# A convolution kernel on one core: the VectorE order of tile 3 interleaved in smaller pieces, and a split matmul taken out of all tiles but one

## The chip, the core and the metric

The kernel runs on one core of a Trainium2 chip. The metric is the device time of one execution in microseconds (us). The engines are TensorE (PE, with its weight loads shown apart as PEld), VectorE (DVE), ScalarE (ACT), GpSimd (POOL) and the DMA queues (SP's and POOL's among them).

## What is computed

The input `x` has 16 images of 256 channels and 56x56 pixels, in fp32.

```
v   = group_norm(x, 32 groups)                   # 8 channels to a group, mean and variance of each
h   = gelu(depthwise_conv3x3(v, dw_weight))      # 9 taps, zero padding
maps = pw_weight @ h + pw_bias                   # 256 -> 8 x 256 channels, for each pixel
out = x + sum_i maps[i] * (roll(v, offset_i) - v)   # 8 directions
```

## The kernel before

An image is worked in 7 tiles of 8 rows (448 pixels), for both halves of the channels (2 x 128). A body covers two images (14 tiles, `nl` from 0 to 13, `t = nl % 7`), and the bodies run one after the other. All engines run the same tiles by hand-written orders, held together by semaphores.

TensorE (`make_maps`) makes the eight direction maps of a tile in 8 units `u`. A unit is two maps ("sides") of 128x448 in two PSUM banks; each map takes six matmuls, since weights and activations are split in a high and a low part (hi x hi, hi x lo, lo x hi, for two halves of the input channels). That is 12 matmuls for a unit, 96 for a tile, 672 for an image. Three units fit in PSUM (MAP_GROUPS = 3), so unit q waits until VectorE has consumed unit q-3: the first wait of `make_maps`, on `prod_s`. The weight load of a matmul is issued ahead of it, so this wait shows at the weight load.

ScalarE (`add_bias`, line 587) scales each map and adds its bias. Between units it also computes gelu for a later tile (line 569), the centre tap that starts a later tile's convolution (`start_conv`, lines 555 and 559), and the cast to the high part (line 574).

VectorE consumes the units: units 0 and 1 by `first_product` (line 702), unit 2 by `second_product` (line 702, in place in PSUM) and `second_add` (line 724, it waits for the product), units 3 to 7 by `kept_product` (line 702, into `products`), which GpSimd adds to the sums (line 363). Between the products VectorE puts in the other eight taps of the convolution of the tile three steps ahead (`tap`, line 784). The seventh tile of an image (SINGLE) holds 8 rows of both channel halves where the others pair two tiles of one half, so its eight taps are sixteen half taps (line 775), two for each call of `tap`. Its taps fall into tile t = 3. Into the same tile (STATS_TILE = 3) fall eleven small operations in nine steps, `group_stats` (lines 656 to 682), which turn the next image's moments into group statistics: each step waits for the one before on VectorE itself. In the last image there is no next image, and tile 3 has no statistics.

VectorE's order in a tile, by `stats_next` (next step of the statistics, nothing where there is none) and `tap_next`, is before: both first products, stats, stats, tap, stats, second product, second add, stats, tap, stats, product 3, stats, tap, stats, product 4, stats, tap, stats, product 5, tap, product 6, tap, tap, product 7, tap. The fourth stats step has two subtractions with the same inputs and different outputs (lines 665 and 666), because the fifth multiplies them with each other (line 669).

TensorE's matmuls are whole (448 columns), but for two places: one matmul of unit 2 in the very first tile (HALVED_FIRST), and one of unit 3 in tile 4 of every image (HALVED) are issued as two matmuls of 224 columns that do the same work.

Of the kernel before, what the change touches and what calls it, by code (L numbers as in the profile page):

```python
# [5 lines left out]
def preact_directional_conv(nc, x, pw_t, pw_b, dw, out):  # L6

    F32, F32R = mybir.dt.float32, mybir.dt.float32r
    ALU, ACT, AX = mybir.AluOpType, mybir.ActivationFunctionType, mybir.AxisListType

    P = 128
    B, C, H, W = x.shape
# [56 lines left out]
    with ctx:  # L69
# [154 lines left out]
        TPAIRS = TILES // 2  # L224
        HALF_STEPS = 2 * SLICES + 2
        MEASURES = HALVES * HALF_STEPS
        STAT = 11
        SCALES = 3
        CONSTS = 5
        PB_SUMS = 5  # L230
# [7 lines left out]
        def upto(table, b0, c):  # L238


            return b0 * sum(table) + ((c // CSTEPS) * sum(table) + sum(table[:c % CSTEPS]))
# [396 lines left out]
        def _(dve):  # L638
            def group_stats(b):


                done = [0]

                def then(ins):
                    ins.then_inc(stat, 1)
                    done[0] += 1

                def wait():

                    dve.wait_ge(stat, b * STAT + done[0])  # L650

                by8 = lambda v: v.rearrange("p (a e) -> p a e", e=GROUP)
                wide = lambda v: window(v, [[1, 32 // GROUP], [0, GROUP]])

                dve.wait_ge(measure, b * MEASURES + MEASURES)
                then(nc.vector.transpose(mom_t[:], moments[:]))
                yield
                wait()
                then(nc.vector.reduce_sum(sums[:], by8(mom_t[:]), axis=AX.X))
                yield  # L660
                wait()
                then(nc.vector.tensor_scalar(by8(mean_t), wide(sums[:]), 1.0 / GROUP, None, ALU.mult))
                yield
                wait()
                then(nc.vector.tensor_tensor(dev_t, mom_t[:], mean_t, ALU.subtract))
                then(nc.vector.tensor_tensor(dev_s[:], mom_t[:], mean_t, ALU.subtract))
                yield
                wait()
                then(nc.vector.tensor_tensor(dev_t, dev_t, dev_s[:], ALU.mult))
                yield  # L670
                wait()
                then(nc.vector.reduce_sum(sums[:], by8(dev_t), axis=AX.X))
                yield
                wait()
                then(nc.vector.tensor_scalar(by8(devs_t), wide(sums[:]), 1.0 / GROUP, None, ALU.mult))
                yield
                wait()
                then(nc.vector.transpose(mean_b[:], mean_t))  # L678
                then(nc.vector.transpose(devs_b, devs_t))  # L679
                yield  # L680
                wait()
                then(nc.vector.scalar_tensor_tensor(var_eps[:], mean_b[:, 1:4:2], EPS, devs_b[:, 0:3:2],
                                                    ALU.add, ALU.add))
                yield
# [49 lines left out]
            def last_tile(n0, nl):  # L734
# [8 lines left out]
                for u in range(HALVES, UNITS):  # L743
# [13 lines left out]
                    if u >= UNITS - HALVES:  # L757
                        dve.wait_ge(prod_s, n * UNITS + u + 1 + PROD0)
                        nc.vector.tensor_tensor(products[:, g, 0, :], a[:, g, 0], a[:, g, 1],
                                                ALU.add).then_inc(final_s, 1)  # L760

            def tap(n0, b0, c, j):


                ip, s, g, t = step_of(c)
                conv = conv_of(n0, c)
                ky, kx = divmod(TAPS_DVE[j], 3)
                if s == SINGLE:
                    for g in range(HALVES):
                        if j == 0:  # L770
                            dve.wait_ge(start_s, upto(START_OF, b0, c) + (g + 1))
                        else:
                            dve.wait_ge(tap_s, upto(TAPS_OF, b0, c) + (2 * (j - 1) + g + 1))
                        d = conv[:, g, :].rearrange("p (r c) -> p r c", c=W)
                        nc.vector.scalar_tensor_tensor(  # L775
                            d, xn[c % 2][:, g * TR + ky:g * TR + ky + ROWS, kx:kx + W],
                            dw_f[:, g, TAPS_DVE[j]:TAPS_DVE[j] + 1], d, ALU.mult, ALU.add).then_inc(tap_s, 1)
                    return
                if j == 0:
                    dve.wait_ge(start_s, upto(START_OF, b0, c + 1))  # L780
                else:
                    dve.wait_ge(tap_s, upto(TAPS_OF, b0, c) + j)
                d = conv.rearrange("p a (r c) -> p a r c", c=W)
                nc.vector.scalar_tensor_tensor(  # L784
                    d, xn[c % 2][:, ky:ky + 2 * ROWS, kx:kx + W].rearrange("p (a r) c -> p a r c", a=2),
                    dw_f[:, g, TAPS_DVE[j]:TAPS_DVE[j] + 1], d, ALU.mult, ALU.add).then_inc(tap_s, 1)
# [56 lines left out]
            def stats_next():  # L843
                for _step in itertools.islice(stats, 1):
                    pass

            def body(n0, b0, last):
                nonlocal stats
                for nl in range(STEPS):
                    t, par = nl % TILES, nl // TILES  # L850
                    taps = iter(range(NT) if not (last and nl + 3 >= STEPS) else ())

                    def tap_next():
                        for j in itertools.islice(taps, 1):
                            tap(n0, b0, nl + 3, j)

                    if last and nl == STEPS - 1:
                        last_tile(n0, nl)
                        return


                    first_product(n0, nl, 0)
                    first_product(n0, nl, 1)
                    if t == STATS_TILE and not (last and par):
                        stats = iter(group_stats(b0 + par + 1))
                    stats_next()
                    stats_next()
                    tap_next()
                    stats_next()
                    second_product(n0, nl)  # L870
                    second_add(n0, nl)
                    stats_next()
                    tap_next()
                    stats_next()
                    kept_product(n0, nl, 3)
                    stats_next()
                    tap_next()
                    stats_next()
                    kept_product(n0, nl, 4)
                    stats_next()  # L880
                    tap_next()
                    stats_next()
                    kept_product(n0, nl, 5)
                    tap_next()
                    kept_product(n0, nl, 6)
                    tap_next()
                    tap_next()
                    kept_product(n0, nl, 7)
                    tap_next()
# [3 lines left out]
        @block.tensor  # L893
        def _(pe):

            HALVED_FIRST = (0, 2, 0, 2)
            HALVED = (4, 3, 0, 2)

            def make_maps(n0, nl, u):

                t, q = nl % TILES, nl * UNITS + u

                need = nl + (1 if t == TILES - 1 else 2)
                wanted = t % 2 == 0


                pe.wait_ge(prod_s, n0 * UNITS + (q - MAP_GROUPS + 1 + PROD0))
                if u == 0 and wanted:
                    pe.wait_ge(hhi_s, n0 + need)
                for side in range(2):  # L910
                    d, g = unit_map(u, side)
                    col = d * C + g * P
                    steps = [(w, hhi, kk) for kk in range(HALVES) for w in (w_hi, w_lo)]
                    steps += [(w_hi, hlo, kk) for kk in range(HALVES)]
                    for s, (w, h, kk) in enumerate(steps):
                        if u == 0 and side == 0 and s == 2 * HALVES and wanted:
                            pe.wait_ge(hlo_s, n0 + need)
                        cuts = (0, PX)
                        if (t, u, side, s) == HALVED or (n0 + nl, u, side, s) == HALVED_FIRST:
                            cuts = (0, PX // 2, PX)  # L920
                        for x0, x1 in itertools.pairwise(cuts):
                            last = nc.tensor.matmul(maps(n0 * UNITS + q)[:, side, x0:x1], w[:, kk, col:col + P],  # L922
                                                    h_part(h, t, nl, kk)[:, x0:x1],
                                                    start=s == 0, stop=s == len(steps) - 1)
                    last.then_inc(maps_s, 1)

            pe.wait_ge(w_lo_s, 1)

            def body(n0, b0, last):
                for nl in range(STEPS):  # L930
                    for u in range(UNITS):
                        make_maps(n0, nl, u)

            run(body)
# [26 lines left out]
```

## Time and profile before

| | us |
|---|---|
| median of 3 runs | 2215.76 |
| lowest, highest | 2214.11, 2215.88 |
| the profiled execution, device time | 2214.68 |
| its span, first to last instruction | 2212.9 |
| busy TensorE, VectorE, GpSimd, ScalarE | 2158.2, 2067.0, 1978.2, 1839.9 |
| mean granted TensorE clock | 0.999 |

The span is 1.8 us shorter than the device time of the same execution. Busy times are sums of instruction durations; a busy TensorE is not TensorE at its peak, and matmuls overlap in the pipeline, so their distance from start to start is what counts, not the duration. All times in the rows count from the span's start.

### The profile page before, as it was taken

To read this page: it belongs to the slowest core of one execution; us is meant where nothing else is said; L and a number is where in the kernel's file an instruction comes from. 1 tells how busy PE (TensorE), PEld (TensorE's weight loads), DVE (VectorE), ACT (ScalarE), POOL (GpSimd) and SP (SyncE) were. 2 spreads that over 40 slices of the span, in tenths; PEclk is the share of its full clock that TensorE was granted. 3 is DMA by queue.
4 is the path that set the end of the run, shared out by engine and by line. 5 is a ranking of instruction groups with operands and counts; after the bars stand their busy time and mean duration, and the time that the engine had idled before them with its cause. 6 is when DMAs were issued, how large, how long until landed. Compare 5 with 4: busy or idle time off the path is not lost.

```text
span 2212.9 us, 28734 instructions
## 1 busy us (share of the span) xinstructions
PE 2158.2 (98%) x10769; PEld 2019.3 (91%) x10769; DVE 2067.0 (93%) x2234; ACT 1839.9 (83%) x2762; POOL 1978.2 (89%) x857
## 2 busy tenths in 40 slices
PE   1999999999999999999999999999999999999998
PEld 1999999999999999999999999999999999999998
DVE  7999999999999999999999999999999999999996
ACT  5979889798887988889788897988879888797775
POOL 5799899899989999899898998999989998999985
PEclk9999999999999999999999999999999999999999
DMA  6245264443725437254462644536354372543424
GB/s 183 48 79 129 48 113 99 89 103 51 157 52 107 92 60 159 34 109 100 70 139 35 124 98 81 114 50 131 79 94 98 60 164 35 108 101 51 100 34 75
DMA packets 47083, 202.13 MB, mean 91 GB/s; under 512 B 3040, under 2 KB 7136, under 8 KB 45664
## 3 DMA queue, kind: packets, MB, share of 16 engines
q0 software_dynamic: 30192, 94.97, 26.3%
q1 hardware_dynamic: 16752, 105.34, 18.6%
q8 instruction: 84, 1.38, 0.3%
q14 instruction: 55, 0.45, 0.1%
HBM read 104.88 MB, written 146.80 MB: 114 GB/s over the span
## 4 chain that ended last, share of the span: by engine, by line
PE 84%; DVE 11%; ACT 2%; issue 2%; DMA 0%; POOL 0%; SPq 0%; DVEq 0%; ACTq 0%
PE psum L922 84%; DVE psum L775 4%; DVE products L702 3%; DVE psum L702 1%; ACT psum L587 1%; DVE psum L784 1%; ACT psum L555 1%; DVE acc L724 1%; ACT hid L569 1%; DMA acc<-x 0%; DVE acc L756 0%; POOL hlo L332 0%; DVE mean_b L678 0%; DVE psum L679 0%; DVE fields L807 0%
## 5 line engine op out<-in xcount | busy, mean ns | idle before, releaser
L587 ACT ACTIVATE psum<-psum,bias,rstd 128x448 f32<-128x448 f32 x1792 | 1200.1, 694 | 323.7 <-PE psum L922 320.5
L922 PE MATMUL psum<-hhi,w_hi 128*128 128x448 f32 x3601 | 1301.9, 362 | 47.0 <-ACT hhi L574 45.3
L363 POOL TENSOR_TENSOR acc<-acc,products 128x896 f32<-128x896 f32 x333 | 1165.8, 3501 | 162.1 <-DVE products L702 150.0
L922 PE MATMUL psum<-hhi,w_lo 128*128 128x448 f32 x3584 | 1300.2, 363 | 0.0
L922 PE MATMUL psum<-hlo,w_hi 128*128 128x448 f32 x3584 | 1009.0, 363 | 0.3 <-POOL hlo L332 0.3
L784 DVE SCALAR_TENSOR_TENSOR psum<-xn,dw_f,psum 128x896 f32<-128x896 f32 x768 | 881.3, 1148 | 72.3 <-ACT psum L559 66.7
L922 PEld LDWEIGHTS psum<-hhi,w_hi 128*128 128x128 f32 x3601 | 676.7, 188 | 97.0 <-issue 45.3
L922 PEld LDWEIGHTS psum<-hlo,w_hi 128*128 128x128 f32 x3584 | 673.2, 188 | 44.9 <-POOL hlo L332 0.9
L922 PEld LDWEIGHTS psum<-hhi,w_lo 128*128 128x128 f32 x3584 | 673.4, 188 | 43.9
L702 DVE TENSOR_TENSOR products<-psum,fields 128x896 f32<-128x896 f32 x555 | 600.6, 1082 | 14.7 <-ACT psum L587 11.1
L332 POOL TENSOR_TENSOR hlo<-hid,hhi 128x896 fp32r<-128x896 f32 x112 | 264.5, 2362 | 12.8 <-ACT hhi L574 12.8
L702 DVE TENSOR_TENSOR acc<-psum,fields 128x896 f32<-128x896 f32 x224 | 241.4, 1085 | 13.8 <-ACT psum L587 12.2
L348 POOL TENSOR_TENSOR fields<-xpad 128x896 f32<-128x896 f32 (+1 forms) x112 | 239.8, 2141 | 0.0
L344 POOL TENSOR_TENSOR fields<-xpad 128x912 f32<-128x912 f32 (+1 forms) x112 | 210.0, 1875 | 0.0
L775 DVE SCALAR_TENSOR_TENSOR psum<-xn,dw_f,psum 128x448 f32<-128x448 f32 x256 | 160.6, 676 | 2.5 <-ACT psum L555 0.5
L702 DVE TENSOR_TENSOR psum<-psum,fields 128x896 f32<-128x896 f32 x117 | 128.6, 1099 | 17.4 <-ACT psum L587 10.1
L370 POOL DMA_DIRECT2D out<-acc x111 | 132.5, 1193 | 7.5 <-DMA out<-acc 6.9
L724 DVE TENSOR_TENSOR acc<-psum,acc 128x896 f32<-128x896 f32 x111 | 121.2, 1092 | 11.9 <-DVE psum L702 0.5
L569 ACT ACTIVATE hid<-psum 128x896 f32<-128x896 f32 x112 | 102.3, 913 | 20.8 <-DVE psum L784 12.6
L540 ACT ACTIVATE xn<-xpad,shift,rstd 128x1008 f32<-128x1008 f32 (+1 forms) x96 | 116.7, 1215 | 0.0
L574 ACT CAST hhi<-hid 128x896 fp32r<-128x896 f32 x112 | 104.8, 935 | 0.0
L559 ACT ACTIVATE psum<-xn,dw_f 128x896 f32<-128x896 f32 x96 | 97.6, 1016 | 8.7
(67 smaller groups left out, 448.2 us busy)
## 6 DMA issues: line engine op xcount, KB each, us to landing
out<-acc POOLq DMA_DIRECT2D x96, 896.0 KB, 7.7
out<-x SPq DMA_DIRECT2D x16, 3136.0 KB, 12.9
xpad<-x SPq DMA_DIRECT2D x30, 1568.0 KB, 14.8
out<-acc POOLq DMA_DIRECT2D x15, 448.0 KB, 5.6
acc<-x SPq DMA_DIRECT2D x4, 784.0 KB, 6.7
xpad<-pw_t SPq DMA_DIRECT2D x1, 2048.0 KB, 12.1
out<-products SPq DMA_DIRECT2D x2, 224.0 KB, 1.9
dw_f<-dw SPq DMA_DIRECT2D x1, 9.0 KB, 8.1
```

Of the source, the lines that this page charges most:

```text
L332: nc.gpsimd.tensor_tensor(hlo[:, slot], hid[:], hhi[:, slot].bitcast(F32), ALU.subtract).then_inc(hlo_s, 1)
L344: nc.gpsimd.tensor_tensor(gx[:, :, f + 2 * lo:f + TR, :], v[:, :, r + 2 * lo:r + TR, 1:WP], v[:, :, r + 2 * lo:r + TR, 0:WP - 1], ALU.subt ...
L348: nc.gpsimd.tensor_tensor(gy[:, :, f + lo:f + ROWS + 1, :], v[:, :, r + lo + 1:r + TR, 1:W + 1], v[:, :, r + lo:r + ROWS + 1, 1:W + 1], AL ...
L363: nc.gpsimd.tensor_tensor(a, a, p, ALU.add).then_inc(added_s, 1)
L370: pool.dma_start(out_dst[b, :, :, t * PX:(t + width) * PX], acc[buf][:, :, sign].rearrange("p g t x -> p g (t x)"), accum_op=ALU.add).then ...
L569: nc.scalar.activation(hid[:], conv_of(n0, c), ACT.Gelu).then_inc(gelu_s, 1)
L587: nc.scalar.activation(m, m, ACT.Identity, bias=bias[ip][:, g, d:d + 1], scale=rstd[ip][:, g:g + 1]).then_inc(biased_s, 1)
L702: return nc.vector.tensor_tensor(to.rearrange("p s (r c) -> p s r c", c=W), maps(n0 * UNITS + q).rearrange("p s (r c) -> p s r c", c=W), f ...
L724: nc.vector.tensor_tensor(a, maps((n0 + nl) * UNITS + u), a, ALU.add).then_inc(prod_s, 1)
L775: nc.vector.scalar_tensor_tensor(d, xn[c % 2][:, g * TR + ky:g * TR + ky + ROWS, kx:kx + W], dw_f[:, g, TAPS_DVE[j]:TAPS_DVE[j] + 1], d, A ...
L784: nc.vector.scalar_tensor_tensor(d, xn[c % 2][:, ky:ky + 2 * ROWS, kx:kx + W].rearrange("p (a r) c -> p a r c", a=2), dw_f[:, g, TAPS_DVE[ ...
L922: last = nc.tensor.matmul(maps(n0 * UNITS + q)[:, side, x0:x1], w[:, kk, col:col + P], h_part(h, t, nl, kk)[:, x0:x1], start=s == 0, stop= ...
```

## The change

Three things are changed. In the single tile (t = 3) the half taps come one at a time: the order up to the second add is now stats, half tap, stats, half tap, stats, half tap, second product, stats, second add, half tap; from there on it is as before, with two half taps for each tap. In the statistics the subtraction is done once, into `dev_s`, and the multiplication squares it: ten operations where there were eleven. The matmul of unit 3 in tile 4 is whole again; the split one in the first tile stays. In other tiles the calls of `stats_next` up to the second add are gone, where they issued nothing.

```diff
-        STAT = 11
+        STAT = 10
...
-                then(nc.vector.tensor_tensor(dev_t, mom_t[:], mean_t, ALU.subtract))
                 then(nc.vector.tensor_tensor(dev_s[:], mom_t[:], mean_t, ALU.subtract))
                 yield
                 wait()
-                then(nc.vector.tensor_tensor(dev_t, dev_t, dev_s[:], ALU.mult))
+                then(nc.vector.tensor_tensor(dev_t, dev_s[:], dev_s[:], ALU.mult))
...
+            def half_tap(n0, b0, c, j, g):
+
+                conv, ky, kx = conv_of(n0, c), *divmod(TAPS_DVE[j], 3)
+                if j == 0:
+                    dve.wait_ge(start_s, upto(START_OF, b0, c) + (g + 1))
+                else:
+                    dve.wait_ge(tap_s, upto(TAPS_OF, b0, c) + (2 * (j - 1) + g + 1))
+                d = conv[:, g, :].rearrange("p (r c) -> p r c", c=W)
+                nc.vector.scalar_tensor_tensor(
+                    d, xn[c % 2][:, g * TR + ky:g * TR + ky + ROWS, kx:kx + W],
+                    dw_f[:, g, TAPS_DVE[j]:TAPS_DVE[j] + 1], d, ALU.mult, ALU.add).then_inc(tap_s, 1)
...
                     def tap_next():
                         for j in itertools.islice(taps, 1):
                             tap(n0, b0, nl + 3, j)
+                        half_tap_next()
+                        half_tap_next()
...
-                    stats_next()
-                    stats_next()
-                    tap_next()
-                    stats_next()
-                    second_product(n0, nl)
-                    second_add(n0, nl)
-                    stats_next()
-                    tap_next()
+                    if single:
+                        stats_next()
+                        half_tap_next()
+                        stats_next()
+                        half_tap_next()
+                        stats_next()
+                        half_tap_next()
+                        second_product(n0, nl)
+                        stats_next()
+                        second_add(n0, nl)
+                        half_tap_next()
+                    else:
+                        tap_next()
+                        second_product(n0, nl)
+                        second_add(n0, nl)
+                        tap_next()
                     stats_next()
                     kept_product(n0, nl, 3)
...
-            HALVED = (4, 3, 0, 2)
...
-                        if (t, u, side, s) == HALVED or (n0 + nl, u, side, s) == HALVED_FIRST:
+                        if (n0 + nl, u, side, s) == HALVED_FIRST:
                             cuts = (0, PX // 2, PX)
```

## Rows read from the trace of the kernel before

**Rows 1.** The page, busy time of each engine over the whole span
```profile
PE 2158.2 (98%) x10769; PEld 2019.3 (91%) x10769; DVE 2067.0 (93%) x2234; ACT 1839.9 (83%) x2762; POOL 1978.2 (89%) x857
```

**Rows 2.** The waits of the whole span: who waited for whom, total, times, longest
```profile
PEld psum L922 <- DVE products L702: 7.2, 15, 0.5
```

**Rows 3.** The chain of waits: start us, us, what (pieces in order of time)
```profile
399.71 115.52 PE psum L922 x577
...
804.18 115.59 PE psum L922 x577
```

**Rows 4.** TensorE timeline, third image: start us, us, form, count, idle before
```profile
399.03 0.56 PE L922 MATMUL psum<-hlo,w_hi 128*128 128x448 f32 x2
399.71 0.47 PE L922 MATMUL psum<-hhi,w_hi 128*128 128x448 f32 x1
400.01 0.36 PE L922 MATMUL psum<-hhi,w_lo 128*128 128x448 f32 x1
...
402.21 0.36 PE L922 MATMUL psum<-hhi,w_hi 128*128 128x448 f32 x1
...
402.61 0.38 PE L922 MATMUL psum<-hhi,w_hi 128*128 128x224 f32 x2
...
403.85 0.36 PE L922 MATMUL psum<-hhi,w_hi 128*128 128x448 f32 x1
```

**Rows 5.** Timeline of the weight loads at the same place
```profile
399.70 0.19 PEld L922 LDWEIGHTS psum<-hhi,w_hi 128*128 128x128 f32 x1 [0.48 <-DVE products L702]
```

**Rows 6.** TensorE timeline, sixth delay: twelve matmuls apart
```profile
804.69 0.37 PE L922 MATMUL psum<-hhi,w_hi 128*128 128x448 f32 x1
...
807.17 0.38 PE L922 MATMUL psum<-hhi,w_hi 128*128 128x224 f32 x2
```

**Rows 7.** TensorE by kind in the window 270 to 390 us
```profile
L922 PE MATMUL psum<-hhi,w_lo 128*128 128x448 f32 x200 | 72.5, 363 | 0.0
```

**Rows 8.** VectorE timeline in tile 3 of the third image
```profile
382.74 1.28 DVE L775 SCALAR_TENSOR_TENSOR psum<-xn,dw_f,psum 128x448 f32<-128x448 f32 x2
383.93 0.18 DVE L662 TENSOR_SCALAR psum<-sums 128x32 f32<-128x32 f32 x1
384.53 1.10 DVE L702 TENSOR_TENSOR psum<-psum,fields 128x896 f32<-128x896 f32 x1 [0.42 <-ACT psum L587]
385.73 1.09 DVE L724 TENSOR_TENSOR acc<-psum,acc 128x896 f32<-128x896 f32 x1
386.74 0.18 DVE L665 TENSOR_TENSOR psum<-mom_t,psum 128x32 f32<-128x32 f32 x1
...
386.93 1.27 DVE L775 SCALAR_TENSOR_TENSOR psum<-xn,dw_f,psum 128x448 f32<-128x448 f32 x2
...
388.22 1.07 DVE L702 TENSOR_TENSOR products<-psum,fields 128x896 f32<-128x896 f32 x1
...
398.58 1.07 DVE L702 TENSOR_TENSOR products<-psum,fields 128x896 f32<-128x896 f32 x1
...
400.76 1.07 DVE L702 TENSOR_TENSOR acc<-psum,fields 128x896 f32<-128x896 f32 x1
```

**Rows 9.** ScalarE timeline in the same tile
```profile
380.43 0.70 ACT L587 ACTIVATE psum<-psum,bias,rstd 128x448 f32<-128x448 f32 x1 [0.50 <-PE psum L922]
...
382.06 1.20 ACT L555 ACTIVATE psum<-xn,dw_f 128x448 f32<-128x448 f32 x2
383.20 1.29 ACT L587 ACTIVATE psum<-psum,bias,rstd 128x448 f32<-128x448 f32 x2
```

**Rows 10.** TensorE timeline: unit 5 of tile 3 starts
```profile
387.43 0.36 PE L922 MATMUL psum<-hhi,w_hi 128*128 128x448 f32 x1
```

**Rows 11.** TensorE timeline at the start of the kernel
```profile
49.80 0.92 PE L922 MATMUL psum<-hlo,w_hi 128*128 128x448 f32 x2
50.54 0.38 PE L922 MATMUL psum<-hhi,w_hi 128*128 128x448 f32 x1
...
53.36 0.38 PE L922 MATMUL psum<-hhi,w_hi 128*128 128x224 f32 x2
```

More of the change, by code:

```diff
@@ L767, in tap @@
                 ky, kx = divmod(TAPS_DVE[j], 3)
[L768 to L778, printed above, removed]
                 if j == 0:
@@ L850, in body, with half_tap_next @@
                     t, par = nl % TILES, nl // TILES
-                    taps = iter(range(NT) if not (last and nl + 3 >= STEPS) else ())
+                    single = (nl + 3) % CSTEPS == SINGLE
+                    taps = iter(range(NT) if not single and not (last and nl + 3 >= STEPS) else ())
+                    half_taps = iter(itertools.product(range(NT), range(HALVES)) if single else ())
+                    def half_tap_next():
+                        for j, g in itertools.islice(half_taps, 1):
+                            half_tap(n0, b0, nl + 3, j, g)
                     def tap_next():
@@ L863, in body @@
                     first_product(n0, nl, 1)
+                    assert single == (t == STATS_TILE)
                     if t == STATS_TILE and not (last and par):
                         stats = iter(group_stats(b0 + par + 1))
-                    stats_next()
-                    stats_next()
-                    tap_next()
-                    stats_next()
-                    second_product(n0, nl)
-                    second_add(n0, nl)
-                    stats_next()
-                    tap_next()
+                    if single:
[14 more added lines that the diff above has]
+                        tap_next()
                     stats_next()
```

## The prediction

> **What bounds the kernel now.** I read the busy times first: TensorE is busy for 98% of the span [rows 1], so nothing that another engine saves counts unless it moves TensorE's stream. So the next view is the waits, and there TensorE's own line. After it has started it waits for VectorE 15 times, 7.2 us in total and never over 0.5 us [rows 2]: once for each image that has statistics to make. The chain of waits says the same: TensorE carries it in pieces of 577 matmuls, one for each image, that begin right behind such a wait [rows 3].
>
> The timeline of the third image shows the place. Matmuls start 0.20 us apart; 601 start between 270 and 390 us, so the pace is 0.2000 us (the row has one of the three kinds, 200 of them, the others have 201 and 200) [rows 7]. The two matmuls from 399.03 on should be followed by one at 399.43, and it starts at 399.71; the next comes 0.30 us behind it instead of 0.20 [rows 4]. The loss is 0.27 + 0.11 = 0.38 us. It is unit 2 of tile 4, whose weight load waited 0.48 us [rows 5] for the product of unit 7 of tile 3, which ends at 398.58 + 1.07 = 399.65 [rows 8]. So VectorE's chain through tile 3, the one tile with sixteen half taps and the statistics, is what is late. From the end of the product to the weight load it is 0.05 us, and in the steady stream the load starts 0.20 us ahead of its matmul, so a product must end about 0.25 us ahead of its matmul to cost nothing. The very next unit shows that 0.38 us is enough: the product it waits for ends at 400.76 + 1.07 = 401.83 [rows 8], and its first matmul starts at 402.21, eleven matmuls and 2.20 us behind 400.01, exactly on pace [rows 4].
>
> A second thing is to be seen in TensorE's stream: it has two paces. After the delay at 804.18 us the matmuls start 2.48 us / 12 = 0.2067 us apart, until the split matmul at 807.17 [rows 6]; from there on it is 0.2000 again. The stretches of the chain with the slow pace in them last 115.59 instead of 115.52 us [rows 3], 4 of the 15; after the other eleven delays the fast pace is back within a few matmuls. So a delay may leave the stream 6.67 ns slow for each matmul, and the split matmul, whatever its reason, stands where the slow pace ends.
>
> **The change, part by part.** All times are those of the third image.
>
> The start of the chain doesn't move. The bias of unit 1 waits for TensorE (0.50 us idle before 380.43), gelu and the two centre taps follow; the two centre taps take 1.20 us from 382.06, so the first ends near 382.7 [rows 9]. The first half tap starts at 382.74 [rows 8]: it waits for that centre tap, and the small steps ahead of it lie in this wait. TensorE sets this time, so everything below can be counted against TensorE's pace.
>
> From there to product 3 it takes 388.22 - 382.74 = 5.48 us now. New: a half tap occupies VectorE for 0.59 us (two in 383.93 - 382.74 = 1.19), a small operation for 0.10 (two from 386.74 to 386.93) [rows 8]. Half tap 382.74, stats 383.34, half tap 383.43 (its centre tap is done at 383.26), stats 384.02, half tap 384.12, second product 384.71. The bias of unit 2 is done at 383.20 + 1.29 = 384.49 [rows 9], so it is no longer waited for; now the product waits for it until 384.53 [rows 8]. The second product gets 0.18 later. The add waits for it: start to start 385.73 - 384.53 = 1.20, against 386.74 - 385.73 = 1.01 behind an operation that nothing waits for [rows 8]. So the fourth small step, put between, fits into that 0.19 and costs nothing; if its cover were gone it would cost 0.10. Add at 385.92, half tap 386.93, stats 387.52, product 3 at 387.62. The gain is 388.22 - 387.62 = 0.60 us: 0.41 of idle time filled by the third half tap, 0.10 hidden behind the second product, 0.10 of the operation removed. The biases of units 3 to 7 leave room: the three that start after the cast end well before, and later ones are paced by TensorE.
>
> From product 3 on the order is the same, so product 7 ends at 399.65 - 0.60 = 399.05. Its matmul is due at 399.43: 0.38 ahead, and 0.25 is needed. The delay of 0.38 us goes, in all 15 images, and unit 3's product is then also earlier against its matmul (0.60 gained, 0.38 given back by the stream). What is next in line: unit 5 of tile 3, which waits for the second add. The add ends at 385.73 + 1.09 = 386.82 now and 387.01 then, its matmul is due at 387.43 [rows 10]: 0.42 ahead. Tile 4's gelu waits for the last half tap, now 0.60 earlier.
>
> The trace has a wait of VectorE for its own last result as 0.19 us of extra distance. The Trainium skill, "VectorE: DVE Perf Modes", section "The DRAIN you can't avoid", says that a semaphore between chained operations costs nothing extra. By that rule the hidden step would gain nothing: product 7 would end 0.28 us ahead of its matmul, and a delay of some images would be as likely as not. The rows speak against it here.
>
> The split matmul: 402.61 to 403.85 holds six matmuls' work and takes 1.24 us [rows 4], so it costs 0.04 us, 16 times. Taking it out also takes out what ends the slow pace. Where no delay comes, no slow pace starts: from the split matmul of the first tile at 53.36 us on [rows 11] this trace keeps 0.2000 to the first delay.
>
> The prologue makes the first statistics on the path to the first matmul: one of two subtractions goes, at the 0.10 us that it takes up in tile 3 [rows 8], once, with nothing beside it. No DMA and no step on SP's or GpSimd's queue moves. GpSimd's power step and its adds get their inputs 0.6 us earlier, and they are not on the chain.
>
> Sum: 15 x 0.38 = 5.7; four slow stretches x 0.07 = 0.3; 16 x 0.04 = 0.6; prologue 0.1; together 6.7 us. On the profiled execution's own 2214.68 that is 2208.0. The median of the runs is 1.1 above that execution and the lowest 0.6 below; since the profiled one lies between them I put the new median at **2208.6**. The unknown part is small: with no gain in the prologue and 0.37 for a delay it is 6.4, with 0.40 it is 7.0, and the runs spread by 1.8.
>
> **The rivals.**
>
> First: the delay stays, smaller, and the slow pace has nothing to end it (slower). It decides at VectorE gaining under 0.47 us in tile 3 where I have 0.60, for instance if half taps beside small steps take longer than in pairs. Then a slow pace lasts from one delay to the next: 656 more matmuls x 6.67 ns = 4.4 us. At the share seen (4 of 15) that is 17.5 us against 0.7 saved: 2214.7 - 0.7 + 17.5 = 2231.5; if every delay fell badly, 2214.7 - 0.7 + 66 = 2280. For it: the reserve is only 0.13 us, and unit 5 of tile 3 has but 0.17. Against it: the 15 delays are alike, and 0.38 cost nothing at unit 3.
>
> Second: the slow pace comes with the clock's rise, not with a delay (slower). Up to 50.54 us matmuls of 448 columns lie 0.37 us apart (two in 50.54 - 49.80), which fits the clock's lower level of 1.2 GHz (448 columns / 1.2 GHz = 0.373) though no row shows a granted clock below full there; from then on they are 0.20 apart, at the upper level of 2.4 GHz, and the split matmul of the first tile stands at 53.36 [rows 11]. If in a run the clock rose behind it, the pace could stay slow: before, the next split matmul at tile 4 ended that (about 400 x 6.67 ns = 2.6 us); now nothing does, and 10,700 x 6.67 ns = 71 us makes 2279. Against it: the split lies 2.8 us behind the rise, and the runs before spread by less than 2.6.
>
> Third: the delays stay in part or whole and the pace stays fast (about the same). With all of them it is 2214.7 - 0.7 - 0.3 = 2213.7, with half 2210.9. The Trainium skill, "TensorE: Matmul & The Clock Gate", section "Wait — 56ns, not 53.3ns?", has one warm distance, columns / 2.4 GHz + 2.5 ns, an estimated 189 ns here. By that rule a delay leaves no trace and a split matmul serves nothing, and this case takes the whole place of the first rival. The rows have 200 and 207 ns, two paces.
>
> **How the numbers follow.** The forecast gets 0.80, the first rival 0.08, the second 0.04, the third 0.08. The forecast's own range is 2207 to 2210; the range reaches to half of the third case, 2206.5 to 2212. A measurement of this kernel can tell about 0.2%, or 4.4 us, from no change: faster means under 2211.3. Faster: 0.80 + half of the third, 0.84; same 0.04; slower 0.12.
>
> **What would show it.** In the profile after: no row of weight loads waiting for VectorE; the chain of waits as one TensorE piece of over 10,000 matmuls; product 7 of tile 3 ending 0.3 to 0.4 us before the matmul of unit 2 of tile 4; second product about 0.2 us later against TensorE and product 3 0.6 earlier; matmuls 0.2000 us apart throughout. The prediction is wrong if a delay of any size is left, above all with 0.2067 us behind it.

## The result: slower, 2234.1 us, and the profile after

The changed kernel takes 2234.09 us (median of 5 runs, 2226.54 to 2240.50) against 2215.54 before (2214.11 to 2215.88). The ratio is 1.0085, with a 95% interval of 1.0072 to 1.0098. The forecast was 2208.6 us, and the delays of TensorE that were to go are twice as many. The profiled execution took 2235.41 us. The mean granted clock was 0.999 in all five runs.

The waits of the whole span of the changed kernel, the lines that answer [rows 2]: who waited for whom, total, times, longest.

```profile
PEld psum L938 <- DVE products L701: 19.2, 30, 0.9
...
DVE psum L769 <- ACT psum L555: 5.6, 15, 0.5
...
PE psum L938 <- DVE products L701: 8.9, 22, 0.5
```

TensorE now waits for VectorE twice in each of 15 images: at unit 6 of tile 3 (for product 3) and at unit 2 of tile 4 (for product 7), where before there was one wait of 0.5 us at most. In the third image, the weight loads show it (start us, us, engine, what; in brackets the wait):

```profile
394.58 0.19 PEld L938 LDWEIGHTS psum<-hhi,w_hi 128*128 128x128 f32 x1 [0.30 <-DVE products L701]
...
404.94 0.19 PEld L938 LDWEIGHTS psum<-hhi,w_hi 128*128 128x128 f32 x1 [0.82 <-DVE products L701]
```

The timeline of VectorE in tile 3 of the third image, which answers [rows 8], shows which step is late; behind it stands GpSimd's timeline at the same place. Columns: start us, us, engine, line, operation, output and inputs.

```profile
387.39 0.69 DVE L769 SCALAR_TENSOR_TENSOR psum<-xn,dw_f,psum 128x448 f32<-128x448 f32 x1 [0.36 <-ACT psum L555]
...
389.36 1.09 DVE L701 TENSOR_TENSOR psum<-psum,fields 128x896 f32<-128x896 f32 x1
390.36 0.18 DVE L665 TENSOR_TENSOR dev_s<-mom_t,psum 128x32 f32<-128x32 f32 x1
390.56 1.09 DVE L723 TENSOR_TENSOR acc<-psum,acc 128x896 f32<-128x896 f32 x1
391.56 0.68 DVE L769 SCALAR_TENSOR_TENSOR psum<-xn,dw_f,psum 128x448 f32<-128x448 f32 x1
392.15 1.38 DVE L668 TENSOR_TENSOR psum<-dev_s 128x32 f32<-128x32 f32 x1
393.45 1.08 DVE L701 TENSOR_TENSOR products<-psum,fields 128x896 f32<-128x896 f32 x1
```

```profile
389.58 1.80 POOL L348 TENSOR_TENSOR fields<-xpad 128x896 f32<-128x896 f32 x1
391.35 2.12 POOL L332 TENSOR_TENSOR hlo<-hid,hhi 128x896 fp32r<-128x896 f32 x1
```

Everything up to the square is as forecast: from the first half tap to the square it is 392.15 - 387.39 = 4.76 us, and the prediction had 387.52 - 382.74 = 4.78. Then the square of 32 numbers (line 668), which the prediction booked at 0.10 us, lasts 1.38 us. It ends at 393.53; GpSimd's subtraction ends at 391.35 + 2.12 = 393.47. In the group view all sixteen squares together take 24.2 us:

```profile
L668 DVE TENSOR_TENSOR psum<-dev_s 128x32 f32<-128x32 f32 x16 | 24.2, 1513 | 0.0
```

The one in the prologue lasts 0.20 us (no GpSimd operation runs there). The other fifteen last 1.0 to 1.9 us, and all fifteen end about 0.06 us behind the end of the GpSimd operation that was running (line 332). The line before, which multiplied a PSUM tensor with an SBUF tensor at the same place, took 0.19 us beside the same GpSimd operation. The half tap at 391.56 reads `xn` and its weights `dw_f` from SBUF, with a PSUM tensor as third input, and takes its usual 0.68 us while the same GpSimd operation runs; `dw_f` gives it one number for each partition and not a second tensor.

The chain of waits, answering [rows 3], shows what the delays do to TensorE's pace (start us, us, matmuls):

```profile
130.16 132.96 PE psum L938 x642
...
812.12 128.92 PE psum L938 x642
...
2032.58 188.76 PE psum L938 x912
```

Pieces of 642 matmuls take 128.92 or 132.96 us, that is 0.2008 or 0.2071 each. The distances of matmul starts over the whole trace say how much each part costs: all distances of the slow pace in stretches (1732 of them, in two long ones of 622 and 934 and some short) cost 1732 x 6.67 ns = 11.6 us, and the 30 delays with the longer distance behind each cost 16.2 us. Together this is 27.8 us.

### The profile page after: what moved, and what is told of

The parts are those of the page before. It is cut to its first block, busy times and chain, and to the rows that moved or that the text cites. A ratio compares the mean times of both kernels' runs of the same rounds, so it can differ in the third digit from the quotient of the medians.

```text
span 2233.6 us, 28686 instructions
## 1 busy us (share of the span) xinstructions
PE 2172.1 (97%) x10753; PEld 2014.1 (90%) x10753; DVE 2083.6 (93%) x2218; ACT 1840.6 (82%) x2762; POOL 1978.2 (89%) x857
## 3 DMA queue, kind: packets, MB, share of 16 engines
q8 instruction: 84, 1.38, 0.3%
## 4 chain that ended last, share of the span: by engine, by line
PE 88%; DVE 9%; ACT 1%; issue 1%; DMA 0%; POOL 0%; SPq 0%; ACTq 0%; DVEq 0%
PE psum L938 88%; DVE psum L769 4%; DVE products L701 2%; DVE psum L784 1%; DVE psum L668 1%; DVE psum L701 0%; DMA acc<-x 0%; ACT hid L569 0%; ACT psum L587 0%; DVE acc L723 0%; ACT psum L555 0%; DVE acc L755 0%; POOL hlo L332 0%; DVE fields L807 0%; DVE part_sums L794 0%
## 5 line engine op out<-in xcount | busy, mean ns | idle before, releaser
L701 DVE TENSOR_TENSOR products<-psum,fields 128x896 f32<-128x896 f32 x555 | 601.3, 1083 | 16.2 <-ACT psum L587 13.1
```

The lines of the kernel that those rows point to most:

```text
L701: return nc.vector.tensor_tensor(to.rearrange("p s (r c) -> p s r c", c=W), maps(n0 * UNITS + q).rearrange("p s (r c) -> p s r c", c=W), f ...
```

## The experiments

The theory from this profile: the square reads two inputs from SBUF and is held until the running GpSimd operation ends; this makes the delays longer; and without the split matmul each delay may leave the slow pace for long. The rivals: the new order or the close spacing of small steps makes VectorE late; the square is slow for another reason; the slow pace costs nothing that a split matmul mends.

**Two subtractions again, new order and whole matmul kept.**

```diff
-        STAT = 10
+        STAT = 11
...
+                then(nc.vector.tensor_tensor(dev_t, mom_t[:], mean_t, ALU.subtract))
                 then(nc.vector.tensor_tensor(dev_s[:], mom_t[:], mean_t, ALU.subtract))
...
-                then(nc.vector.tensor_tensor(dev_t, dev_s[:], dev_s[:], ALU.mult))
+                then(nc.vector.tensor_tensor(dev_t, dev_t, dev_s[:], ALU.mult))
```

> The changed kernel with the old statistics: two subtractions again, and the product of the PSUM copy with the SBUF copy. The order in half taps and the whole matmul stay. Theory (the square of an SBUF tensor with itself takes two SBUF inputs and waits for the GpSimd instruction that runs, 1.0 to 1.9 us in the trace after): the multiplication lasts 0.19 us again, product 3 comes 0.6 us earlier than before, all 15 delays go, time 2207.5 to 2210. Rival (the new order itself, or waits between close small steps, makes VectorE late): the delays stay as in the changed kernel, 2226 to 2240.

Measured: 2207.79 us (7 runs, 2207.04 to 2208.76) beside 2214.33 before, ratio 0.9971 (0.9960 to 0.9982). The profiled execution took 2207.58. The one operand makes the difference between 2234 and 2208. Its chain of waits is one piece of TensorE, and its VectorE timeline in the third image has the multiplication at its old length beside the same GpSimd operation:

```profile
47.17 2146.35 PE psum L939 x10725
```

```profile
383.41 1.09 DVE L702 TENSOR_TENSOR psum<-psum,fields 128x896 f32<-128x896 f32 x1
384.41 0.18 DVE L665 TENSOR_TENSOR psum<-mom_t,psum 128x32 f32<-128x32 f32 x1
384.50 0.18 DVE L666 TENSOR_TENSOR dev_s<-mom_t,psum 128x32 f32<-128x32 f32 x1
384.61 1.09 DVE L724 TENSOR_TENSOR acc<-psum,acc 128x896 f32<-128x896 f32 x1
385.62 0.68 DVE L770 SCALAR_TENSOR_TENSOR psum<-xn,dw_f,psum 128x448 f32<-128x448 f32 x1
386.20 0.19 DVE L669 TENSOR_TENSOR psum<-psum,dev_s 128x32 f32<-128x32 f32 x1
386.30 1.08 DVE L702 TENSOR_TENSOR products<-psum,fields 128x896 f32<-128x896 f32 x1
```

```profile
385.38 2.13 POOL L332 TENSOR_TENSOR hlo<-hid,hhi 128x896 fp32r<-128x896 f32 x1
```

Both subtractions fit between the second product and the add: add 1.20 us behind the product, as with no step between [rows 8]. The changed kernel's profiled execution is 2235.4 - 2207.6 = 27.8 us longer than this one, which is what the delays and the slow pace add up to above.

**The square alone, in the kernel before.** The edit is the statistics part of the change by itself: STAT 10, the first subtraction gone, `dev_s` multiplied with itself.

> The kernel before with the one-subtraction statistics alone; old order, the split matmul in every image kept. Theory: the square starts 0.68 to 1.25 us ahead of the end of GpSimd's split of h and lasts that long plus 0.06, so VectorE is 0.5 to 1.0 us later in tile 3 and each of 15 delays grows from 0.38 by that; with the split matmul there the slow pace stays under 50 matmuls an image. 2215.5 + 15 x 0.75 = 2227, range 2222 to 2232. Rival (the square costs nothing by itself): 2215.

Measured: 2227.16 us (4 runs, 2226.26 to 2227.69), ratio 1.0057 (1.0044 to 1.0070). In the third image the square lasts 0.83 us, until 0.06 behind GpSimd's end at 388.84 + 2.12 = 390.96. It lasts 0.83 us in seven images, 1.40 in seven and 1.13 in one. TensorE waits at weight loads 30 times, 19.5 us.

```profile
390.19 0.83 DVE L668 TENSOR_TENSOR psum<-dev_s 128x32 f32<-128x32 f32 x1
```

```profile
388.84 2.12 POOL L332 TENSOR_TENSOR hlo<-hid,hhi 128x896 fp32r<-128x896 f32 x1
```

**The changed kernel with the split matmul back.**

```diff
+            HALVED = (4, 3, 0, 2)
...
-                        if (n0 + nl, u, side, s) == HALVED_FIRST:
+                        if (t, u, side, s) == HALVED or (n0 + nl, u, side, s) == HALVED_FIRST:
```

> The changed kernel with the split matmul of unit 3 in tile 4 of every image back. Theory (two paces): the profiled execution of the changed kernel had 1732 matmuls at 0.2067 us, 11.6 us of its time, in two long stretches of 622 and 934; with the split matmul no stretch is longer than about 60 matmuls, so about 11 us less and 0.6 more for the split: 2222 to 2226, and the runs spread by less than 3 us instead of 14. Rival (the split matmul does nothing but cost 0.04 us): 2234, with the same spread.

Measured: 2227.26 us (5 runs, 2226.50 to 2227.76), ratio 1.0057 (1.0045 to 1.0069). The spread fell from 14 us to 1.3, as expected of the two paces. The median was expected at 2222 to 2226 and lies above: in the profiled execution the slow stretches still cost 1.7 us, where 0.04 x 16 = 0.6 for the splits was all that I had added. It equals the experiment before it, which differs in the order alone, and the two traces show why: the new order brings VectorE to the square earlier, but the square ends with the same GpSimd operation, and all that follows counts from there. In the third image the square ends at 390.19 + 0.83 = 391.02 with the old order and the delayed matmul of tile 4 starts at 402.43; with the new order it ends at 388.62 + 1.36 = 389.98 and the matmul starts at 401.40, 11.41 and 11.42 us behind.

```profile
388.62 1.36 DVE L668 TENSOR_TENSOR psum<-dev_s 128x32 f32<-128x32 f32 x1
```

```profile
401.40 0.47 PE L939 MATMUL psum<-hhi,w_hi 128*128 128x448 f32 x1 [0.33 <-DVE products L701]
```

**The kernel before without the split matmul.** The reverse of that edit, on the kernel before.

> The kernel before without the split matmul of unit 3 in tile 4; all else as before. Theory: 15 delays of 0.38 us stay, and each leaves the slow pace for 656 more matmuls, 4.4 us, with a chance of about 4 in 15: 2215.5 - 0.6 + 17.5 = 2232, range 2219 to 2250, with runs some us apart. Rival (one pace): 2214.9, runs within 2 us.

Measured: 2260.20 us median of 7 runs from 2223.92 to 2277.02. (The ratio of 1.013 that comes with it, 1.0085 to 1.0175, leaves out the four longest of them, so the runs themselves are what to read.) The slow pace is there, and worse than expected. The chain of waits of its profiled execution (2260.2 us):

```profile
533.78 115.51 PE psum L921 x576
668.60 1577.55 PE psum L921 x7632
```

After the fifth delay the slow pace came and stayed for the rest, 7652 distances, 51 us. There is no sixth delay: all waits of weight loads for VectorE are five, 2.4 us. At 0.2067 us a tile takes 96 x 6.67 ns = 0.64 us longer, more than the 0.48 that TensorE waited [rows 5], so VectorE is not late again, and no delay comes that could give the fast pace another chance. The trace bears this out: in the ten later images with statistics product 7 ends 0.42 us ahead of its matmul, where the prediction needs 0.25. The rows are those of the eleventh image (1500.46 + 1.09 = 1501.55, matmul at 1501.97). The granted clock from 700 to 2200 us is 1.00, as in the same stretch of the kernel before, so the slow pace is not a lower clock. That the runs differ by when the stream falls into the slow pace fits this, but only one of them has a trace.

```profile
1500.46 1.09 DVE L702 TENSOR_TENSOR products<-psum,fields 128x896 f32<-128x896 f32 x1
```

```profile
1501.97 0.37 PE L921 MATMUL psum<-hhi,w_hi 128*128 128x448 f32 x1
```

**Two SBUF copies against one SBUF and one PSUM copy.** Both kernels have the new order, two subtractions and the split matmul in every image. They differ in where the first subtraction writes. The reference:

> The new order with two subtractions as in the first experiment, and the split matmul in every image too. With no delay there is no slow pace for the split to end, so all it does is cost 0.04 us 16 times: 2207.8 + 0.6 = 2208.4, within 2207.5 to 2209.5. It is also the reference for the next one, which differs in one operand. Rival (the split matmul saves something even without a delay): under 2207.

Measured: 2208.51 us (7 runs, 2208.22 to 2209.81) beside 2215.20 before, ratio 0.9971 (0.9960 to 0.9981); no wait of TensorE for VectorE. Its median is 0.7 us above that of the first experiment, but the two ran on different occasions, and each is about as far below its own before (6.7 and 6.5 us). The traces tell what 16 splits cost: from the split in the first tile to the start of the last matmul it is 2198.85 - 53.19 = 2145.66 us here and 2197.94 - 52.91 = 2145.03 in the first experiment, 0.63 more, and 16 x 0.04 is 0.64.

The other kernel differs from it so:

```diff
+        dev_u = sb("dev_u", [P, 32])
...
-                then(nc.vector.tensor_tensor(dev_t, mom_t[:], mean_t, ALU.subtract))
+                then(nc.vector.tensor_tensor(dev_u[:], mom_t[:], mean_t, ALU.subtract))
...
-                then(nc.vector.tensor_tensor(dev_t, dev_t, dev_s[:], ALU.mult))
+                then(nc.vector.tensor_tensor(dev_t, dev_u[:], dev_s[:], ALU.mult))
```

> The same, but both subtractions write SBUF tensors, and two different SBUF tensors are multiplied. Theory (a VectorE operation with two SBUF inputs waits for the running GpSimd operation, whatever they are): the multiplication lasts 1.0 to 1.9 us, ending about 0.06 us behind GpSimd's split of h, 30 waits of TensorE, 2226 to 2228 as the changed kernel with the split back. Rival (it is reading one tensor through both inputs that is slow, or reading what was just written): 2208.4.

Measured: 2227.77 us (4 runs, 2227.38 to 2228.00), ratio 1.0056 (1.0041 to 1.0072). Two different tensors, and the same wait, to the same end. So it is not the squaring of one tensor:

```profile
390.16 1.35 DVE L670 TENSOR_TENSOR psum<-dev_u,dev_s 128x32 f32<-128x32 f32 x1
```

```profile
389.33 2.12 POOL L333 TENSOR_TENSOR hlo<-hid,hhi 128x896 fp32r<-128x896 f32 x1
```

**One subtraction, without a second SBUF input.**

```diff
-                then(nc.vector.tensor_tensor(dev_s[:], mom_t[:], mean_t, ALU.subtract))
+                then(nc.vector.tensor_tensor(dev_t, mom_t[:], mean_t, ALU.subtract))
...
-                then(nc.vector.tensor_tensor(dev_t, dev_s[:], dev_s[:], ALU.mult))
+                then(nc.vector.tensor_tensor(dev_t, dev_t, mom_t[:], ALU.mult))
```

> The changed kernel with one subtraction, into PSUM, multiplied with the SBUF moments instead of with itself: since deviations of a group sum to zero, the sum of deviation times value is the sum of squared deviations. Ten operations, and one SBUF input beside a PSUM one. Theory: this is what the prediction described, 2207.5 to 2208 (0.1 us of the prologue less than with two subtractions); the multiplication lasts 0.19 us and no wait of TensorE for VectorE is left. Rival (something in the count of operations or their spacing matters): over 2212.

Measured: 2207.73 us (5 runs, 2207.52 to 2207.97), ratio 0.9967 (0.9954 to 0.9979). The multiplication lasts 0.19 us:

```profile
386.47 0.19 DVE L668 TENSOR_TENSOR psum<-psum,mom_t 128x32 f32<-128x32 f32 x1
```

That no wait is left holds but for one: in the eleventh image the second add starts 0.36 us late, for no reason that the profile shows, and the weight load of unit 5 of tile 3, which the prediction had named as next in line, waits 0.17 us for it:

```profile
1461.57 0.19 PEld L938 LDWEIGHTS psum<-hhi,w_hi 128*128 128x128 f32 x1 [0.17 <-DVE acc L723]
```

This kernel has all that the change set out to do, and it and the first experiment beat both kernels. Between these two no difference can be told.

**No split matmul anywhere, no delay.** The first experiment, with the split of the first tile taken out as well.

> The first experiment (two subtractions, no delay left) without the split matmul of the first tile. Theory (the clock's rise leaves either pace, and without a split or a delay it stays to the end): profiles so far show the slow pace between the clock's rise and the first split in 3 of 6 executions. So about half the runs near 2207.5 and about half near 2207.8 + 10,740 x 6.67 ns = 2279, nothing between. Rival (only delays bring the slow pace, or it ends by itself): all runs within 2 us of 2207.8.

Measured: six runs: 2207.60, 2207.88, 2208.00, 2208.39, 2208.42 and 2279.06 us. The sixth value is within 0.4 us of the forecast for a whole kernel at the slow pace, and there is nothing between. The share was one in six instead of half; six runs don't fix it. The profiled execution was one of the quick ones, so no trace shows the long one: that it is the slow pace rests on its length and on the traces above. Its mean granted clock was 1.000, so a lower clock did not make it long. In the nine profiled executions that have the split of the first tile, the pace between what the prediction calls the clock's rise (where the distances go from 0.37 to 0.20 us) and that split was slow in four.

## Why the prediction was wrong

**What bounds the kernel** was read rightly: a delay of 0.38 us at one place, for product 7 of tile 3, and two paces. The first experiment removed the delays and landed at 2207.8 where the forecast was 2208.6; it is 6.5 us less than its own before, where the sum had 6.7.

**The step that failed** is "stats 387.52, product 3 at 387.62": I priced the new multiplication at the 0.10 us of every small operation, by rows of operations that had at most one SBUF input. The change removed "0.10 of the operation removed" and, with it, the PSUM copy that was the second operand. The runs showed 1.0 to 1.9 us instead, the rest of a GpSimd operation of 2.1 us. From the first half tap to product 3 the third image now takes 393.45 - 387.39 = 6.06 us, where it took 5.48 before and 4.88 was forecast. So VectorE was 0.6 us later where it was to be 0.6 earlier. This put a new delay at unit 6 of tile 3, and longer ones at tile 4: 16.2 us in place of 5.7.

The Trainium skill states this, and I did not weigh it: "SBUF — State Buffer", section "Who interferes with whom", has a VectorE instruction with two SBUF inputs contend with a GpSimd instruction that reads SBUF, since the second input comes through an interface that both share, and the later one waits for the other to finish. The traces agree: in the changed kernel all fifteen ends lie about 0.06 us behind GpSimd's, and so do the fifteen in each of the other three traces with two SBUF inputs. In all of them the GpSimd operation is the same one, the subtraction that makes `hlo`; no run tries another.

The trace of the kernel before has what fits it, from the other side, in rows that the prediction did not use. In the prologue VectorE joins the weights, SBUF with SBUF, and GpSimd's small operations beside it are long:

```profile
18.96 1.03 POOL L320 TENSOR_TENSOR rstd<-var_eps,neg_half 128x2 f32<-128x2 f32 x1 [6.28 <-DVE var_eps L682]
20.07 0.60 POOL L323 TENSOR_TENSOR shift<-mean_b,rstd 128x2 f32<-128x2 f32 x1
20.64 0.66 POOL L324 TENSOR_TENSOR bias<-pb_f,rstd 128x16 f32<-128x16 f32 x1
```

The same three take 0.71, 0.19 and 0.21 us in tile 3:

```profile
123.55 0.71 POOL L320 TENSOR_TENSOR rstd<-var_eps,neg_half 128x2 f32<-128x2 f32 x1 [1.70 <-DVE var_eps L682]
124.34 0.19 POOL L323 TENSOR_TENSOR shift<-mean_b,rstd 128x2 f32<-128x2 f32 x1
124.50 0.21 POOL L324 TENSOR_TENSOR bias<-pb_f,rstd 128x16 f32<-128x16 f32 x1
```

**The order** was right term by term. The second product comes 0.2 later, steps between it and the add are free, and the chain from the first half tap to the step after is 4.76 us against 4.78. With the old operands, product 7 ends 0.39 us ahead of its matmul (396.67 + 1.08 = 397.75, matmul at 398.14 in the third image) where 0.38 was forecast:

```profile
396.67 1.08 DVE L702 TENSOR_TENSOR products<-psum,fields 128x896 f32<-128x896 f32 x1
```

```profile
398.14 0.36 PE L939 MATMUL psum<-hhi,w_hi 128*128 128x448 f32 x1
```

So the hidden small step is hidden, as the rows had said. The Trainium skill's rule that a semaphore between chained operations costs nothing extra ("VectorE: DVE Perf Modes", section "The DRAIN you can't avoid"), which the prediction cites, does not hold at this place: 1.20 us from start to start with the wait, 1.01 without it [rows 8].

**The first rival** came true in its second half, a slow pace that nothing ends. Its first half had a smaller delay left, from half taps beside small steps; the delays grew instead, and by the square. Its price was mis-sized too. I let the slow pace last from one delay to the next, 4.4 us; with delays of 0.38 us it ends the delays too and stays, 51 us in the trace of the kernel before without its split. With the longer delays of the changed kernel VectorE is late even for the slow stream, so each delay decides the pace anew, and the slow one costs 11.6 us. Forecast for this case: 2231.5; measured: 2234.1. That the two are near is luck: the rival had 17.5 us of slow pace with no new delays, the profiled execution has 11.6 of it and 10.5 more of delays (16.2 - 5.7).

**The second rival**, a slow pace from the clock's rise on, has its start shown by the four traces above. That the clock is what rises there is inferred from the distances: the granted clock of the kernel before is 1.00 on both sides (45 to 49 and 51 to 60 us). That it can last to the end rests on the length of one run of six, 2279.06 against the 2279 worked out, and it showed only once the first tile's split was gone too. The changed kernel keeps that split, and in its profiled execution the split did end a slow pace, at 52.60 us.

**The third rival**, delays without a lasting slow pace, is ruled out by the same runs: taking out one split matmul for each image moved the kernel before by 46 us (2260.20 - 2214.33). The Trainium skill's rule of one warm distance ("TensorE: Matmul & The Clock Gate", section "Wait — 56ns, not 53.3ns?"), which the prediction cites, does not allow that.

## What to carry to other kernels

A second copy of a small tensor in PSUM beside the one in SBUF is not waste: count for each VectorE operation how many of its input tensors lie in SBUF, and look at what GpSimd does at that moment; an operation of 0.2 us was held here for up to 1.9 us of a GpSimd operation of 2.1. And before an odd piece such as a split matmul is taken out, find out in the trace what differs ahead of it and behind it, and what would end that state in its place. The parts do not add up: alone in the kernel before, the square costs 12.8 us (2227.16 - 2214.33) and the whole matmul 46, while the order alone gains 6.7 (2215.20 - 2208.51). Beside the square the order gains nothing (2227.26 against 2227.16), and the whole matmul costs about 7 (2234.09 - 2227.26, on different occasions), because the longer delays decide the pace anew again and again. With no delay left the whole matmul saves 0.6.

## What the runs showed of the hardware that I had not expected

- A VectorE multiplication of 128x32 with two SBUF tensors as inputs ended about 0.06 us behind the end of the GpSimd operation that was running (the subtraction that makes `hlo`, 2.1 us), 60 times of 60 in four traces. With one of the inputs in PSUM it took 0.19 us beside the same operation.
- Matmuls of 448 columns, each with its own weight load, run 0.2000 or 0.2067 us apart, both at a granted clock of 1.00. The slow pace begins at a delay or where the distances fall from 0.37 to 0.20 us near 50 us, not each time, and can stay for thousands of matmuls (7652 in one trace); in the nine traces with split matmuls there are 89 splits; 16 stand in the slow pace, and all 89 have the fast pace behind them. What in the chip makes the two paces stays open.
- The slow pace can keep itself alive: in the trace of the kernel before without its split it gives the other engines 0.64 us for each tile, and so takes away the very delays that could end it (ten images of ten with no delay).
